# A decoder's second mixture of experts: the shared experts of one token group moved behind the routed blocks, gathers with fewer blankings between them, and a reordered drain

## The reference

```python
def _L1_ffn_ref(hidden_states, w_gate, w1_e, w3_e, w2_e, w1_s, w3_s, w2_s):
    x = hidden_states.reshape(-1, H)                  # 2048 tokens, 256 channels
    weights, idx = _gate(x, w_gate)                   # 4 of 16 experts for each token
    combine = (jax.nn.one_hot(idx, E, dtype=x.dtype) * weights[..., None]).sum(1)
    g = jax.nn.silu(jnp.einsum('th,efh->tef', x, w1_e))
    u = jnp.einsum('th,efh->tef', x, w3_e)
    routed = jnp.einsum('tef,ehf,te->th', g * u, w2_e, combine)
    shared = _swiglu(x, w1_s, w3_s, w2_s)             # every token
    return (routed + shared).reshape(shape)
x = _layernorm(x + _L1_attn_ref(x, ...), axis=-1)
x = _layernorm(x + _L1_xattn_ref(x, ctx_1024, ctx_1024, mask, ...), axis=-1)
x = _layernorm(x + _L1_ffn_ref(x, ...), axis=-1)
```

## Time and profile before

| | |
|---|---|
| median of three runs | 1320.81 us (1320.22 to 1320.89) |
| the profiled execution | 1321.61 us, its span 1319.4 us |
| busy, of the span | PE 88%, PEld 63%, DVE 53%, ACT 44%, POOL 36% |
| recurrent stage, then mixture | from about 924, then 1077 to 1319 us |

### The profile page before, as it was taken

How to read it: one execution, slowest core, us unless ns; L and a number is a source line. 1 busy time by engine, 2 the same in 40 slices (tenths; PEclk the granted TensorE clock), 3 DMA queues, 4 the chain that set the end, 5 groups by cost and what they waited for, 6 DMA issues and landing times. The chain is left out here.

```text
span 1319.4 us, 23829 instructions
## 1 busy us (share of the span) xinstructions
PE 1157.6 (88%) x7558; PEld 836.2 (63%) x7558; DVE 697.9 (53%) x1882; ACT 586.9 (44%) x1071; POOL 474.6 (36%) x948
## 2 busy tenths in 40 slices
PE   7799898999978868999999999998789769999970
PEld 4344444444344435889999999987455556999940
DVE  4766666766255643422222323267677637554664
ACT  3277677777755634222333333231443122557710
POOL 7355332231432331013332323211342265716456
PEclk9599999999988988999999999999798759999995
DMA  9900200000000007301111111040800014867633
GB/s 347 351 1 13 86 0 1 0 0 1 1 0 1 1 1 303 150 25 34 40 37 37 37 37 39 27 136 1 274 1 1 12 69 131 259 194 240 205 118 102
DMA packets 68128, 109.32 MB, mean 83 GB/s; under 512 B 7345, under 2 KB 54962, under 8 KB 65202
## 3 DMA queue, kind: packets, MB, share of 16 engines
q1 hardware_dynamic: 58130, 80.96, 18.0%
q0 software_dynamic: 9888, 27.01, 6.4%
HBM read 65.61 MB, written 42.34 MB: 82 GB/s over the span
## 5 line engine op out<-in xcount | busy, mean ns | idle before, releaser
L1421 ACT ACTIVATE f_work<-f_bank,f_ub 128x128 f32<-128x128 f32 x312 | 89.0, 368 | 204.3 <-PE f_bank L1743 204.3
L496 ACT ACTIVATE att_PT<-att_ST 128x1024 f32<-128x1024 f32 (+1 forms) x192 | 148.1, 809 | 64.2 <-PE att_ST L634 32.7
L541 DVE CUSTOM_DVE_ANT_0 att_junk<-att_RB,att_causal_q 128x128 f32<-128x128 f32 (+3 forms) x256 | 120.7, 488 | 58.0 <-PE att_RB L616 49.0
L1743 PEld LDWEIGHTS f_bank<-f_work,f_xTf 128*128 128x128 f32 x1248 | 145.3, 192 | 3.9 <-DVE f_work L1543 2.0
L1743 PE MATMUL f_bank<-f_work,f_xTf 128*128 128x128 f32 x1248 | 145.8, 275 | 1.5 <-DVE f_work L1543 1.5
L1752 PE MATMUL f_bank<-wd_down,f_work 128*128 x624 | 141.1, 379 | 0.0
L616 PE MATMUL att_RB<-att_kT,att_qT 96*128 96x512 bf16 (+3 forms) x384 | 120.4, 351 | 22.0 <-DVE att_mx L541 6.6
L1752 PEld LDWEIGHTS f_bank<-wd_down,f_work 128*128 128x128 f32 x624 | 115.5, 190 | 14.1
L1372 POOL DMA_INDIRECT Yd<-f_work,f_inv x39 | 38.5, 987 | 196.3 <-DVE f_work L1562 196.3
L1552 DVE COPY f_xTf<-wu_up 128x1024 f32 x78 | 54.1, 695 | 102.6 <-PE f_bank L1743 94.9
L616 PEld LDWEIGHTS att_RB<-att_kT,att_qT 96*128 96x128 bf16 x384 | 34.0, 98 | 112.9 <-issue 41.2
(11 more groups left out here) (460 smaller groups left out, 2188.1 us busy)
## 6 DMA issues: line engine op xcount, KB each, us to landing
Xd<-g_zero SPq DMA_DIRECT2D x1, 12032.0 KB, 41.2
f_xin<-Xd SPq DMA_DIRECT2D x47, 256.0 KB
Yd<-f_yo SPq DMA_DIRECT2D x47, 256.0 KB, 2.6
wu_up<-up_w SPq DMA_DIRECT2D x9, 1024.0 KB, 9.3
wd_down<-down_w SPq DMA_DIRECT2D x9, 1024.0 KB, 18.4
w_all<-w SPq DMA_DIRECT2D x6, 768.0 KB, 10.6
wu_up<-Yd SPq DMA_DIRECT2D x16, 256.0 KB, 6.0
w_all<-w SPq DMA_DIRECT2D x1, 2304.0 KB, 17.2
```

What stands on the lines that cost most here:

```text
L496: act.activation(buf[:, :, 0:w], ST[:, 2 * (k % 2):2 * (k % 2) + 2, 0:w], ACT.Exp, scale=float(HD) ** -0.5).then_inc(exp_done, 1)
L541: dve.tensor_tensor_reduce(junk[:, k % RING, 0:w], RB[:, bank, 0:w], G.causal_q[:, 512 - w:512], 1.0, LOWEST, ALU.add, ALU.max, to).then_i ...
L1421: last = act.activation(hT[:, u % 2, m, :], bank[:, UB + m // 4, (m % 4) * P:(m % 4 + 1) * P], ACT.Gelu, bias=ub[:, ds(e, 1), m])
L1743: mm = pe.matmul(bank[:, UB + n, P * m:P * (m + 1)], staged_up[:, kk, at:at + P], xT[:, u % 2, kk, :], start=(kk == 0), stop=(kk == KD - 1))
```

## The change

In the recurrent stage, the count `ct` moves from behind the second `r` step of the last quarter to between the two, and `locate` with the first three scatters from behind the `rs` steps to right behind the second `r`, so ahead of `dn`, `rs` and `o`. `spread_of` no longer computes the shift for the mixer's norm (n = 1), and computes the negative mean ahead of the power for the others. In the mixture, one shared group instead of two (AHEAD = 1) is computed before the blocks. The group of tiles 4 to 7 (LATE_SUMS) follows behind the blocks: its routed rows are added to x, and its shared result last, and the moments of these tiles are taken after that. In the second half's gathers, the memset stays behind every other gather of the first three tiles and is left out elsewhere; `spread(1)` stands behind the third tile's gathers. The order of the drain's PE and DVE steps is new.

```diff
--- before.py
+++ after.py
@@ -1837,8 +1837,8 @@
 
     put(("tx", 2, 1), ("tg", 0, 0), ("tg", 0, 1), ("tg", 1, 0), ("tg", 1, 1))
     put(("v", 3, 1), ("lg", 0, 0), ("c", 0, 0), ("c", 0, 1), ("c", 0, 2), ("c", 0, 3))
-    put(("r", 3, 1), ("ct", 0, 0))
-    put(("rs", 3, 1), ("lc", 0, 0), ("sx", 0, 3))
+    put(("r", 3, 0), ("ct", 0, 0))
+    put(("r", 3, 1), ("lc", 0, 0), ("sx", 0, 3))
     put(("y", 3, 1), ("sx", 3, 13))
     return plan
 
@@ -1958,9 +1958,12 @@
 
                 pool.wait_ge(var_ready[n], k)
                 ch.link(pool.tensor_scalar(rstd[n][p][:, j], mv[n][p][:, j, 1], LN_EPS, None, ALU.add))
-                ch.link(pool.tensor_tensor(rstd[n][p][:, j], rstd[n][p][:, j], half[:, j], ALU.pow))
-                ch.link(pool.tensor_tensor(shift[n][p][:, j], mv[n][p][:, j, 0], rstd[n][p][:, j], ALU.mult))
-                pool.tensor_scalar(shift[n][p][:, j], shift[n][p][:, j], -1.0, None, ALU.mult).then_inc(rstd_ready[n], 1)
+                if n == 1:
+                    pool.tensor_tensor(rstd[n][p][:, j], rstd[n][p][:, j], half[:, j], ALU.pow).then_inc(rstd_ready[n], 1)
+                else:
+                    ch.done(pool.tensor_scalar(shift[n][p][:, j], mv[n][p][:, j, 0], -1.0, None, ALU.mult))
+                    ch.link(pool.tensor_tensor(rstd[n][p][:, j], rstd[n][p][:, j], half[:, j], ALU.pow))
+                    pool.tensor_tensor(shift[n][p][:, j], shift[n][p][:, j], rstd[n][p][:, j], ALU.mult).then_inc(rstd_ready[n], 1)
 
             ch.done(pool.memset(half[:, :], -0.5))
             pool.memset(one[:, :], 1.0)
@@ -2469,7 +2472,7 @@
     NX = 4
     NG = NT // J
     SCATTERS, SENT = TH * K, 13
-    FIRST = NG // 2
+    FIRST, AHEAD = NG // 2, 1
     CE = TH * E
     Xd, Yd = a["Xd1"], a["Yd1"]
     w13, w2, gate = W.w13, W.w2, W.gate
@@ -2486,6 +2489,7 @@
     staged_up = staged[:, :, :, 0:W.UPW].rearrange("p b i (k f) -> p b i k f", k=KD)
     staged_down = staged[:, :, :, W.UPW:W.UPW + D]
     LATE = LAST[0] + 6
+    LATE_SUMS = (1,)
     yo = sb("yo", [P, 2, 2, D])
     gs = sb("gs", [P, 2, 512])
     hs = sb("hs", [P, 2, 2, 512])
@@ -2575,8 +2579,9 @@
                             pool.wait_ge(up_ready, LAST[0] + 2 + (K * s + r) // 2)
                         pool.indirect_dma_start(ga[:, s, r, :], None, Yd[0:P * R * (n + 1), :],
                                                 bass.IndirectOffsetOnAxis(pos[:, n, r, s:s + 1], 0)).then_inc(gathered[s], 16)
-                        ch.pause(route.rest[:, 0:16])
-                    if n and s == 0:
+                        if n == 0 or (s < 3 and r % 2):
+                            ch.pause(route.rest[:, 0:16])
+                    if n and s == 2:
                         spread(1)
                     if n and s == 5:
                         spread(2)
@@ -2612,7 +2617,7 @@
 
             for q in range(3):
                 stage(q)
-            for m in range(2 * FIRST):
+            for m in range(2 * AHEAD):
                 shared_silu(m)
 
             def silu(q):
@@ -2638,7 +2643,7 @@
                 if q and q + 2 < N:
                     stage(q + 2)
             result(N - 1)
-            for m in range(2 * FIRST, 2 * NG):
+            for m in range(2 * AHEAD, 2 * NG):
                 shared_silu(m)
 
         @block.vector
@@ -2655,11 +2660,12 @@
                 tt(hs[:, i % 2, s, :], gs[:, s, :], bank[:, 2 * s + 1, :], ALU.mult).then_inc(sh_prod, 1)
 
             def shared_sum(i):
+                to = G.x_sb if i not in LATE_SUMS else acc
                 for b in range(2):
                     t = J * i + 2 * b
                     dve.wait_ge(sh_y, 2 * i + b + 1)
                     tt(acc[:, t:t + 2, :].rearrange("p t c -> p (t c)"), bank[:, YB + b, :],
-                       G.x_sb[:, t:t + 2, :].rearrange("p t c -> p (t c)"), ALU.add).then_inc(sh_added, 1)
+                       to[:, t:t + 2, :].rearrange("p t c -> p (t c)"), ALU.add).then_inc(sh_added, 1)
 
             for i in range(FIRST, NG):
                 dve.wait_ge(turned[1], i - FIRST + 1)
@@ -2693,10 +2699,13 @@
 
             def weigh(n, s, r):
                 t = TH * n + s
+                late = t // J in LATE_SUMS
                 if r == 0:
                     dve.wait_ge(gathered[s], 16 * K * (n + 1))
-                    dve.wait_ge(sh_added, t // 2 + 1)
-                ins = dve.scalar_tensor_tensor(acc[:, t, :], ga[:, s, r, :], wgt[:, n, s, r:r + 1], acc[:, t, :],
+                    if not late:
+                        dve.wait_ge(sh_added, t // 2 + 1)
+                base = G.x_sb if late and r == 0 else acc
+                ins = dve.scalar_tensor_tensor(acc[:, t, :], ga[:, s, r, :], wgt[:, n, s, r:r + 1], base[:, t, :],
                                                ALU.mult, ALU.add)
                 ch.link(ins)
                 if r == K - 1:
@@ -2725,14 +2734,11 @@
             route.choose(dve, ch, 1, 2)
             shared_product(1)
             route.choose(dve, ch, 1, 3)
-            shared_product(2)
             dve.wait_ge(sums_ready, 1)
             route.locate(dve, ch, 1, bank[:, SB_ + 1, 0:CE], bank[:, SB_ + 1, CE:2 * CE])
             shared_sum(0)
-            shared_product(3)
             take_x(0)
             take_x(1)
-            shared_sum(1)
             route.owners(dve, ch, 1)
             FROM = [LAST[0] + 7 + at for at in (0, 3, 5, 8, 11, 13, 15)]
             when = {FROM[s] + part: (s, part) for s in range(TH - 1) for part in range(2)}
@@ -2748,19 +2754,25 @@
                     s, part = when[q]
                     weigh(0, s, 2 * part)
                     weigh(0, s, 2 * part + 1)
-                    if part:
+                    if part and s < J * AHEAD:
                         measure(s)
-            shared_product(4)
+            shared_product(2)
             norm(0)
-            shared_product(5)
+            shared_product(3)
             for r in range(K):
                 weigh(0, TH - 1, r)
-            measure(TH - 1)
+            shared_product(4)
+            shared_sum(1)
+            shared_product(5)
+            dve.wait_ge(sh_added, 4)
+            for t in range(J * AHEAD, TH):
+                measure(t)
+            shared_sum(2)
             shared_product(6)
-            shared_sum(2)
-            shared_product(7)
             for s in range(TH):
                 if s == 1:
+                    shared_product(7)
+                if s == 3:
                     norm(1)
                 if s == 2:
                     shared_sum(3)
@@ -2853,7 +2865,7 @@
                 if q >= 2:
                     pe.wait_ge(y_done, q - 1)
                 else:
-                    pe.wait_ge(sh_added, 2 * (FIRST - 1) + q + 1)
+                    pe.wait_ge(sh_added, 2 * (AHEAD - 1) + q + 1)
                 for i in range(2):
                     mm = pe.matmul(bank[:, YB + p, i * D:(i + 1) * D], hT[:, p, i, :], staged_down[:, q % 3, i, :],
                                    start=True, stop=True)
@@ -2864,14 +2876,11 @@
             score()
             shared_up(0)
             shared_up(1)
-            shared_up(2)
+            shared_down(0)
             count()
-            shared_down(0)
-            shared_up(3)
-            pe.wait_ge(sh_prod, 2 * FIRST)
+            pe.wait_ge(sh_prod, 2 * AHEAD)
             turn_x(0)
             turn_x(1)
-            shared_down(1)
             up(0)
             turn_x(2)
             for q in range(1, N):
@@ -2882,11 +2891,14 @@
             down(N - 1)
             pe.wait_ge(xt_done, N)
             pe.wait_ge(ht_done, N)
+            shared_up(2)
+            shared_up(3)
             shared_up(4)
+            pe.wait_ge(y_done, N)
+            shared_down(1)
             shared_up(5)
+            shared_down(2)
             shared_up(6)
-            pe.wait_ge(y_done, N)
-            shared_down(2)
             shared_up(7)
             shared_down(3)
     sc.close()
```

## The result

| | before | after |
|---|---|---|
| median of five runs | 1320.89 us (1320.22 to 1322.16) | 1309.73 us (1306.20 to 1312.99) |
| ratio | | 0.9916, interval 0.9895 to 0.9938 |
| span of the profiled execution | 1319.4 us | 1309.4 us |

What follows compares the result with a forecast made beforehand. PE was taken to bound the kernel through the block steps, then POOL's gathers. Recurrent stage -7.0, lead-in -3.6, clock +3.0 and drain -3.2 sum to -10.8: 1320.8 to 1310.0 us, range 1304.5 to 1315.5.

Steps and rivals of the forecast that it cites:

- Part 1, the deviation step: Recurrent-stage tails: norm waits only for the power; 0.75 us in each of three tails, 0.2 in the last.
- Part 2, `locate` and three scatters earlier: Third quarter's plan in the recurrent stage: POOL's queue starts sooner, so the last `x4` comes 4.6 us earlier.
- The bound of 3.4 from the scatters' shift: Lower bound for the last `x4` in the recurrent stage: only the scatters' shift of 3.4 us arrives.
- Rival (b): Recurrent stage: the last `y` is delayed, gain only the 1.4 us by which `o` moves; 1313.2 us, chance 0.15.
- Part 3, the lead-in: Before the blocks: one shared group less, then the wait for block step 0's rows; `up(0)` 3.6 us earlier.
- Part 3, the clock: First block steps: PE idle about 6 us ahead of them, so they run at half clock; 3.0 us lost.
- Rival (a): Clock not lost in the wait for rows, or gained in the recurrent stage's shorter idle; 1307.0 us, chance 0.18.
- Part 4, the drain: Behind the blocks: POOL's gathers without memsets stay last, 1.30 us each; 3.2 us gained.
- B: Time mark from which the drain is counted: the end of the last `down` of the blocks.
- Rival (c): Drain: gathers without memsets cost 1.55 us each; 1314.5 us, chance 0.13.
- Rival (e): Drain: PE's delayed shared group takes over the end, so nothing is gained there; about 1321 us, chance 0.04.
- Rival (d): Drain: without memsets gathers queue up and POOL stalls; 1326.2 us at 2.2 us a gather, chance 0.06.

Runs made afterwards that it cites:

- e3: Kernel before with only both recurrent-stage edits (shorter deviation step; count, locate and three scatters earlier), mixture as before: 1320.42 us, ratio 0.9959.
- e2: Changed kernel with both recurrent-stage edits undone, the mixture staying changed: 1319.24 us, ratio 0.9946.
- e4: Kernel before with the shorter deviation step alone: 1321.58 us, ratio 0.9969.
- e1: The changed kernel timed again without edits, on the first chip: 1315.25 us, ratio 0.9924 to the kernel before.
- e5: Changed kernel with eleven unused matmul calls filling PE's wait for the first block rows: 1309.66 us, ratio 0.9918 to the kernel before.
- e8: Changed kernel with no memset behind any of the second half's gathers: 1308.60 us, ratio 0.9920 to the kernel before.
- e10: Kernel before with only the count, locate and three scatters moved earlier: 1327.97 us, ratio 0.9986.
- e11: Changed kernel with one more shared_up before the blocks, no memsets in the second half's gathers, one filler matmul call: 1320.85 us, ratio 0.9931 to the kernel before.
- e12: As e11, with the deviations of tiles 4 to 9 in one call instead of two: 1328.67 us, ratio 1.0001 to the kernel before.
- e9: Changed kernel with five unused matmul calls in PE's wait ahead of block step 0: 1320.24 us, ratio 0.9931 to the kernel before.
- e7: Changed kernel with a memset back behind each of the second half's gathers: 1310.26 us, ratio 0.9930 to the kernel before.
- e6: Changed kernel with one shared_up of the second token group moved into PE's wait, products and silus reordered: 1307.93 us, ratio 0.9904 to the kernel before.

## Why the prediction was right, step by step

The time was 1309.73 against 1310.0. That it lies this close is in part luck. The five times of the changed kernel are spread over 6.8 us, and in the ledger the errors cancel: 3.4 us too much for the recurrent stage and nothing for the 1.4 us that the second profile gained ahead of it by chance (that mark lies between 925.2 and 929.0 us over all profiles), 0.6 too much for the lead-in, 1.7 too much for the clock's loss. In time the stage's edits alone gave 5.4 us (e3) for a forecast of 7.0, and the mixture's alone 7.1 (5.0 to 9.2, e2) for one of 3.8; the ledger has 4.9 for the mixture. The steps hold to different degrees.

**Part 1, the deviation step: the mechanism right, the tails a little too high.** `x4` starts behind the power. Where the clock took the same course, two tails gave 1.2 us (above, e4), so 0.6 each for a forecast of 0.75: it is the lower bound, and what the second call gains by starting earlier does not show. The 1.9 of e4 after three tails has another course of the clock in it. But the edit also gives 1.5 in the last tail, where I had it at 0.2, since I had counted the shorter calls of `y` with part 2.

**Part 2, `locate` and three scatters earlier: right in what it does, its size holds only with part 1.** Together the two edits brought the last `x4` earlier by 6.0 to 7.8 us from the stage's start in e1, e3 and e5 to e8 (forecast 7.0), and the stage by 6.7 to 7.8. Alone, the move gave 2.3 of the 4.6 from the stage's start (e10), or 2.8 counted from the third tail's last `x4`; 1.3 to 1.6 of the difference are the shorter calls of part 1. Counted from that same `x4`, the last one comes 4.4 us earlier in e1, near the 4.6. The bound of 3.4 from the scatters' shift was nearer to the move by itself, and still too high. Rival (b) had 1.4 us and the last `y` as what releases `x4`. The releaser is still POOL, so its mechanism fell. Its price is nearer to e10's time of 1.9 us (0.3 to 3.5) than the bound is, by luck.

The result's own profile has only 3.6 of the 7.0. POOL's queue seems to run as forecast, three scatters to 1045.15 and the `y` calls to 1050.4, but 1.4 us of that lie ahead of the stage. Two things are missing. The third tail's last `x4` came 0.9 us earlier and not 2.0 to 3.4. And behind it `locate` came only 1.4 us earlier and not 3.1 as in e1 and e10, since the clock fell sooner in the last quarter. PE's logits there, before and then after (timelines):

```profile
1022.10 3.64 PE L2251 MATMUL rx_R<-w_gate,r_xTf 128*128 128x16 f32 x32
```

```profile
1019.78 4.50 PE L2254 MATMUL rx_R<-w_gate,r_xTf 128*128 128x16 f32 x32
```

They take 4.50 us instead of 3.64 (3.64 in e1 too), and the count comes 21.1 us behind that `x4`, against 19.4 in e1. Of the ten profiles with both edits, seven have 6.7 to 7.8, and three have 3.5 or 3.6 (the result's, e11, e12); these three were granted 0.83 in 980 to 990 where the others' low windows lie elsewhere. So the stage's gain is 7 us at one course of the clock and 3.6 at another, and which one an execution gets is not the kernel's doing alone, as e1 shows. None of these is a gain at an equal clock: the profiles of before, e2 and e10 share a course of their own, which none of the ten has. The gains in time, 5.4 (e3) and 2.9 (e2), are of that size and don't tell the two apart. The forecast gave one number where the clock makes two.

**Part 3, the lead-in: 3.0 for 3.6.** PE's wait was 5.94 us for a forecast of about 6. The load landed 2.97 us after its issue and not 2.4, which is the 0.6. It was the term for which before had no row, within its bounds of 1.6 and 3.4; no run shows the 1.6. The 0.5 us that the half clock costs on the turn lie in this stretch too, and are made up for by the 1.8 us from turn to `up`, which are 1.38 at full clock (e5).

**Part 3, the clock: the mechanism right, the size wrong.** It fell before the rows landed and came back at 1107.7, 4.4 us behind the turn, within the 3.5 to 6.2. The failed step is "0.5 us on the turn, and 3.5 to 6.2 us of block work at half speed, half of which is lost": e5 puts the sum at 1.3 to 1.7. The 0.5 on the turn is right (1.87 against 1.38 in e5). But the 4.4 us until the clock came back start with the turn, and not with the first `up`, so only 2.5 us of block work ran at half clock, and 1.2 of them were lost (3.07 against 1.89). Rival (a), no loss, fell. What I wrote for it, that idle times of 2.3 us elsewhere kept the full clock, is a wrong reading: the profile of before has five idle times of PE between 1.9 and 2.9 us, one of them the 2.31 us ahead of 1043.75, and behind each the granted clock goes to 1.2 GHz within 4 us.

**Part 4, the drain: right to the tenth, as a sum.** B + 50.6 was forecast for the last `weigh` and measured (50.9 to 51.2 in e1, e2, e5 and e9). Its terms: second row of gathers at B + 21.8 (22.2), the deviation step 2.2 (2.2), 18 gathers at 1.32 (1.30), landing 2.9 (2.7). The shares are another matter: the forecast's terms give 1.6 us to the memsets (18 x 0.09) and 1.4 to the second row's earlier start (23.6 to 22.2). With all memsets back the row starts as early, at B + 21.85, and yet the drain is 61.1, so in the profiles the memsets own 2.9 of the 3.2 and the order 0.3. In time e7 and e8 are 1.7 us apart, which doesn't settle it. Rival (c), 1.55 a gather, is the first of a row only (1.40). Rival (e) fell: the late shared group ends far ahead of the last gather.

**Rival (d), a stall without memsets, was given 0.06 and a mechanism in which gathers slow down.** They never did: 1.25 apart in each kernel, single ones 1.4 to 1.5. But on one chip the other engines stood still beside them in e11 and e12, and in e12 the whole gain was gone. The changed kernel keeps six memsets and doesn't show it. That the memsets are the reason is not shown.

**What stays open:** why ACT and DVE take results of PE up to 12 us late beside a long row of gathers, and why on one chip only; and whether filling PE's wait without a second one behind it gives the 1.5 us, since e5 overshot and e9 had the second wait.

## What to carry to other kernels

When two edits act on the same queue, a forecast of their sum can be right while each one's share is not: price them together, and say which of them owns a shared term. Before work is added to fill an engine's wait, look at the next wait behind it, since the clock falls there as well. And take small pauses out of a row of software DMAs only as far as the row sets the end: those ahead of a wait were free, and in two kernels without any of them, which had another order too, other engines stood still on one of two chips.

## What the runs showed of the hardware

- Back-to-back indirect DMAs on POOL mostly start 1.25 to 1.27 us apart (0.95 and a gap of 0.30), with a memset between them 1.35; single ones take 0.1 to 0.2 more in either form (e7, e8).
- Behind an idle time of 2.65 us on PE (e6), and behind one of 2.28 that followed two turns of 1.04 us together (e9), the granted clock went to 1.2 GHz within the next 2 us; in the result's profile it came back after 4.4 us of dense work.
- A matmul call of 512 fp32 columns is two passes of 0.43 to 0.45 us each at 2.4 GHz (22 in 9.66 us in e5, 10 in 4.51 in e9).
- Two chips differ. The kernel before takes 6 to 9 us longer on one of them, and there ACT waited 11.7 us in eight waits of its L2628 within the blocks without a releaser in the profile (e1), none in the result's. The Trainium skill ("SBUF — State Buffer", SBUF: two separate sides) says that within the engines' side only the port pair shared by DVE and POOL causes contention, and ACT never waits for it. In e12 ACT's read of PE's bank comes 12 us behind PE's end; the rule speaks of the ports of SBUF, and so it neither explains nor excludes what the trace shows.
